# Packing the count stage's places two words to a stride, and dividing them apart on the engine

## The chip, the core and the metric

The kernel runs on one core of one Trainium2 chip. Its time is device microseconds from launch to the end of the program; a profiled execution gives beside it a span, from the first to the last recorded instruction. The engines are PE (TensorE, matrix multiplication; its weight loads are listed apart, as PEld), DVE (VectorE), ACT (ScalarE), POOL (GpSimd) and SP (SyncE, which issues DMAs). Each engine has a sequencer that reads its instructions in order. Register arithmetic and loads of registers run on that sequencer; the profile lists them under the engine's name with a q (PEldq, ACTq) and doesn't count them as busy time.

## The reference

Four graph layers run over one graph of 3125 nodes and 103,125 edges, sorted by destination. Each layer normalizes the node rows, applies a ReLU and adds its result to `x`:

```python
edge_index = jnp.stack([src, dst])
h = jnp.maximum(_layernorm(x, axis=-1), 0.0)
x = x + _L0_gnn_ref(h, edge_index, ...)        # gated messages summed over the edges, then a GRU
h = jnp.maximum(_layernorm(x, axis=-1), 0.0)
x = x + _L1_gnn_ref(h, edge_index)             # three hops of scatter-mean
h = jnp.maximum(_layernorm(x, axis=-1), 0.0)
x = x + _L2_gnn_ref(h, src, dst, ...)          # mean over the neighbours, then an MLP
h = jnp.maximum(_layernorm(x, axis=-1), 0.0)
x = x + _L3_gnn_ref(h, edge_index, ...)        # attention over the edges, feed-forward
return x
```

Layers 0 to 2 sum over the edges, as in

```python
msg_sum = jax.ops.segment_sum(feat[src], dst, num_segments=n)
```

and such a sum is a product with the matrix of counts, whose element for two nodes is the number of edges from one to the other. The kernel builds that matrix once, from `src` and `dst`.

## The kernel before

The program runs in blocks, one after the other, and an engine enters a block when all have left the one before. `tables` (L423) computes index tables on the chip. `count_matrix` (L679) builds the matrix of counts: this is the count stage. Then come the layers.

**The count stage.** The edges lie in 806 tiles of 128. The destinations are cut into windows of 5 nodes. A step is one tile against one window that it touches, and there are 1431 steps. For one step, PE multiplies a 128x128 matrix that is 1 where an edge's source has a given low part by a 128x125 matrix that is 1 where its destination in the window and the high part of its source match (L762). The product is added into a slot of PSUM of 128 f32 words that stands for the window. PSUM holds 32 slots (8 banks of 4), in 4 pairs of banks with 8 slots each. Eight steps are a stride (`STRIDE`), and there are 179 strides.

Three engines work on it side by side. DVE compares the tables for 16 steps at a time (L725, two instructions for two strides) and writes into a ring of three. PE takes, for each stride, first two one-column products that clear the flags of the pair of banks that comes next (`clear`, L740), and then the stride's eight products. ACT copies one finished pair of banks, 8 slots, from PSUM to `counts` for each stride (L769). PE waits at the head of stride j until ACT has made its first j - 1 copies. ACT waits until PE has counted stride j and until its own copy before is done.

**Which slot a step goes to depends on the data.** So the addresses stand in a table in SBUF, and the engine loads them into registers: `values` (L116 to L121) becomes one register load that fetches a run of words. The table is made in `CountTables.places` (L364 to L392) by DVE, inside `tables`, on one partition. `AHEAD` strides share a fetch. Before, `AHEAD` is 3: 27 words, filled up to 28, are fetched for three strides, in 60 fetches. 24 of them are ready addresses (slot number times 128), 3 are the pair to clear, times 1024. In front of each product, the sequencer turns a word into an address (a FUSED_REGOPS instruction, several register operations in one). ACT has a table of its own (`c_out`), with the pair in the high half of a word and the column in the low half, loaded 8 words at a time by `Registers.take`.

PE's loop: the fetch and the products stand in one queue, in the order of the code, with no fetch ahead of its first use.

Of the kernel before, what the change touches and what calls it, by code (L numbers as in the profile page):

```python
# [30 lines left out]
AHEAD = 3  # L31
# [186 lines left out]
class CountTables:  # L218
# [7 lines left out]
    def __init__(self, k, scope):  # L226
        s = k.s
        n, cols = s.csteps, s.nb * s.w
        self.k = k

        def sb(name, shape, dt=F32):
            return k.sb(scope, name, shape, dt, "right")
        self.key, self.low = sb("c_key", [P, n + 1], F16), sb("c_low", [P, n + 1], F16)


        self.fetches = -(-s.strides // AHEAD)
        self.words = -(-AHEAD * (STRIDE + 1) // 4) * 4
        self.place = sb("c_place", [1, self.fetches, self.words], I32)
        self.out = sb("c_out", [1, self.fetches * AHEAD], I32)
        self.lows, self.keys = sb("low_table", [P, P, 2], F16), sb("key_table", [P, cols, 2], F16)  # L240

    def stage(self, scope):
# [6 lines left out]
        def sb(name, shape, dt=F32):  # L249
            return k.sb(scope, name, shape, dt)  # L250
# [13 lines left out]
        self.window = sb("c_window", [1, whole], I32)  # L264
# [98 lines left out]
    def places(self, e):  # L363
# [3 lines left out]
        assert STRIDE * PAIRS == 32 and SLOT == 128  # L367
        wide = STRIDE * s.w
        every = AHEAD * STRIDE
        e.memset(self.place[:, :, every + AHEAD:], 0).then_inc(*v.up())  # L370
        e.tensor_scalar(self.place[:, :, 0:every], self.window[:, :].rearrange("p (a b) -> p a b", b=every),
                             STRIDE * PAIRS - 1, 7, ALU.bitwise_and, ALU.logical_shift_left).then_inc(*v.up())
# [3 lines left out]
        for to, more in ((self.clear, 1), (self.pair, PAIRS - 1)):  # L376
# [5 lines left out]
        e.tensor_scalar(self.place[:, :, every:every + AHEAD], self.clear[:, :].rearrange(  # L382
            "p (a b) -> p a b", b=AHEAD), PAIRS - 1, 10, ALU.bitwise_and, ALU.logical_shift_left).then_inc(*v.up())
# [8 lines left out]
        e.tensor_tensor(self.out[:, :], self.column[:, :], self.pair[:, :], ALU.bitwise_or).then_inc(*v.up())  # L392

# [285 lines left out]
def count_matrix(k, c, counts, room, nodes, w_nodes, factors):  # L679
# [10 lines left out]
    with ExitStack() as scope:  # L690
# [12 lines left out]
        flat = k.psum[:, :, :].rearrange("p b n -> p (b n)")  # L703

        with k.nc.Block() as block:
# [32 lines left out]
            def _(e):  # L738
                def clear(bank):
                    return e.matmul(bank, none[:, 0:P], none[:, 0:1], start=True, stop=True, skip_group_check=True)  # L740
                words = c.place[0:1, :, :].rearrange("p a b -> p (a b)")
                last_slot = (STRIDE * PAIRS - 1) * SLOT
# [5 lines left out]
                for j in range(s.strides):  # L748
                    if j % AHEAD == 0:
                        at = j // AHEAD * c.words  # L750
                        fetched = k.values(ENGINE.PE, words, at, at + c.words, last_slot)
                    place = fetched[j % AHEAD * STRIDE:(j % AHEAD + 1) * STRIDE]
                    ahead = fetched[AHEAD * STRIDE + j % AHEAD].with_bounds(min_val=0, max_val=(PAIRS - 1) * 1024)
                    if j >= 2:
                        e.wait_ge(copied.sem, copied.at(j - 1))
                    for i in range(2):
                        clear(flat[:, 512 * i + 511:][:, bass.ds(ahead, 1)])
                    if j % per == 0:
                        e.wait_ge(hots.sem, hots.at(2 * (j // per) + 2))
                    for i in range(j * STRIDE, min(s.csteps, (j + 1) * STRIDE)):  # L760
                        hot = (slice(None), i // keep % ring, i % keep // 2, slice(None), i % 2)
                        last = e.matmul(flat[:, bass.ds(place[i - j * STRIDE], cols)], lows[hot], keys[hot], start=False, stop=True,  # L762
                                        skip_group_check=True)
# [3 lines left out]
            def _(e):  # L767
# [6 lines left out]
                for j in range(s.strides):  # L774
                    if j % 8 == 0:
                        out = outs.take(j)
                    pair = (out[j % 8] >> 16).with_bounds(min_val=0, max_val=PAIRS - 1)
                    column = (out[j % 8] & 0xffff).with_bounds(min_val=0, max_val=wide * (s.fills - 2))
# [1989 lines left out]
```

## Time and profile before

| what | value |
|---|---|
| time, median of 3 runs | 2528.77 us (2525.51 to 2531.3) |
| span of the profiled execution | 2249.7 us |
| median less span: launch and what lies around the span | 279.1 us |
| mean granted clock of TensorE | 0.829 |
| the count stage, in the span | 75 to 417.6 us |

The profiled execution has no time of its own beside its span; the difference of 279.1 us to the median of the runs stands in for what lies around it. In the rows below, times are microseconds from the span's start. "Idle before, releaser" is what ended the time in which an engine did nothing. The granted clock is a share of 2.4 GHz: 0.50 is 1.2 GHz.

### The profile page before, as it was taken

To read this page: it belongs to the slowest core of one execution; us is meant where nothing else is said; L and a number is where in the kernel's file an instruction comes from. 1 tells how busy PE (TensorE), PEld (TensorE's weight loads), DVE (VectorE), ACT (ScalarE), POOL (GpSimd) and SP (SyncE) were. 2 spreads that over 40 slices of the span, in tenths; PEclk is the share of its full clock that TensorE was granted. 3 is DMA by queue.
4 is the path that set the end of the run, shared out by engine and by line. 5 is a ranking of instruction groups with operands and counts; after the bars stand their busy time and mean duration, and the time that the engine had idled before them with its cause. 6 is when DMAs were issued, how large, how long until landed. Compare 5 with 4: busy or idle time off the path is not lost. (4 is left out here: it accounts for less than half of the span.)

```text
span 2249.7 us, 34161 instructions
## 1 busy us (share of the span) xinstructions
PE 1665.0 (74%) x10041; PEld 1359.7 (60%) x10041; DVE 1504.7 (67%) x3141; ACT 969.8 (43%) x2263; POOL 916.3 (41%) x880
## 2 busy tenths in 40 slices
PE   5566666899799999865667677766777767776756
PEld 2455555655478887634566666666666656666744
DVE  4766666577744342477677777867777867787875
ACT  0355565677455234430234434434434335344535
POOL 1000000000100000037777777777777777777800
PEclk9555555799999999988788988888888898898877
DMA  2100000000034000034333333333343333333211
GB/s 70 60 1 1 1 1 1 8 0 0 29 87 130 27 1 6 14 100 96 92 90 91 97 93 91 92 96 92 87 100 94 86 95 97 91 93 93 60 39 29
DMA packets 134433, 136.86 MB, mean 61 GB/s; under 512 B 28689, under 2 KB 105074, under 8 KB 134258
## 3 DMA queue, kind: packets, MB, share of 16 engines
q0 software_dynamic: 27776, 60.71, 12.2%
q1 hardware_dynamic: 106482, 73.98, 11.5%
q8 instruction: 90, 1.47, 0.3%
q14 instruction: 85, 0.70, 0.1%
HBM read 129.67 MB, written 4.92 MB: 60 GB/s over the span
## 5 line engine op out<-in xcount | busy, mean ns | idle before, releaser
L2112 POOL DMA_INDIRECT rows<-x_l,src x856 | 896.9, 1048 | 292.5 <-issue 260.1
L2180 PE MATMUL psum<-both,node_hot 128*128 128x144 f32 x1712 | 304.1, 332 | 202.0 <-DVE both L2374 175.2
L2180 PEld LDWEIGHTS psum<-both,node_hot 128*128 128x128 f32 x1712 | 264.7, 222 | 229.4 <-issue 197.4
L2127 PE MATMUL psum<-w_e,edges 128*128 128x272 f32 x856 | 323.9, 466 | 56.7 <-DVE z L2287 46.9
L2129 PEld LDWEIGHTS psum<-x_r,hot 128*128 128x128 f32 x1712 | 313.8, 224 | 51.1
L2129 PE MATMUL psum<-x_r,hot 128*128 x1712 | 313.1, 312 | 0.0
L2287 DVE TENSOR_TENSOR z<-psum,rows 128x544 f32<-128x544 f32 x214 | 154.3, 721 | 235.4 <-issue 163.7
L2237 ACT ACTIVATE apart<-iota,minus_rel 128x128 f32<-128x128 f32 x828 | 261.9, 386 | 0.0
L769 ACT ACTIVATE counts<-psum (+1 forms) x181 | 181.5, 1003 | 175.8 <-PE psum L762 112.1
L1145 POOL TENSOR_TENSOR ht<-ht,mix_rows 128x512 f32<-128x512 f32 (+1 forms) x7 | 7.8, 1149 | 587.4 <-ACT mix_rows L1186 587.4
L1260 PE MATMUL psum<-halves,counts 128*128 128x257 f16 (+1 forms) x1725 | 198.1, 277 | 7.4 <-DVE halves L1465 3.9
L762 PE MATMUL psum<-keys,x 128*128 128x125 f16 x1431 | 201.3, 283 | 0.4
L2127 PEld LDWEIGHTS psum<-w_e,edges 128*128 128x128 f32 x856 | 160.7, 228 | 62.4 <-DVE hot L2280 31.2
L1260 PEld LDWEIGHTS psum<-halves,counts 128*128 128x128 f16 (+1 forms) x1725 | 171.2, 100 | 34.3 <-DVE halves L1465 4.5
L725 DVE TENSOR_TENSOR x<-low_table,c_low 128x2048 f16<-128x2048 f16 x90 | 109.6, 1218 | 116.0 <-PE psum L762 114.6
L762 PEld LDWEIGHTS psum<-keys,x 128*128 128x128 f16 x1431 | 148.3, 104 | 25.8 <-issue 1.6
L2392 DVE TENSOR_TENSOR acc<-acc,psum 128x144 f32 x428 | 128.6, 300 | 44.9 <-PE psum L2180 8.0
L2233 ACT ACTIVATE both<-weight 128x64 f32<-128x64 f32 x214 | 52.9, 247 | 235.7 <-PE psum L2180 232.8
L2300 DVE TENSOR_REDUCE alpha<-z 128x32 f32<-128x544 f32 x214 | 152.5, 713 | 1.5 <-issue 0.3
L2293 DVE SCALAR_TENSOR_TENSOR z<-z,att 128x512 f32<-128x512 f32 x214 | 146.5, 685 | 1.1
L2374 DVE TENSOR_TENSOR both<-rows,weight 128x512 f32<-128x512 f32 x214 | 143.9, 680 | 0.2 <-ACT weight L2224 0.2
L740 PE MATMUL psum<-none 128*128 128x1 f16 x366 | 57.1, 183 | 105.7 <-ACT counts L769 102.1
(335 smaller groups left out, 2187.3 us busy)
## 6 DMA issues: line engine op xcount, KB each, us to landing
rel_row<-e_rel_rows SPq DMA_DIRECT2D x107, 256.0 KB
edges<-edge_t SPq DMA_DIRECT2D x428, 32.0 KB
rows<-x_l,src POOLq DMA_INDIRECT x856
edge_part<-edge_t SPq DMA_DIRECT2D x40, 320.0 KB, 3.1
x_r<-x_l SPq DMA_DIRECT2D x1, 1632.0 KB
ht<-x SPq DMA_DIRECT2D x6, 256.0 KB, 2.8
new<-e_new_before SPq DMA_DIRECT2D x12, 128.0 KB
new<-e_new_behind SPq DMA_DIRECT2D x12, 128.0 KB
```

The lines of the kernel that those rows point to most:

```text
L762: last = e.matmul(flat[:, bass.ds(place[i - j * STRIDE], cols)], lows[hot], keys[hot], start=False, stop=True, skip_group_check=True)
L769: return e.activation(counts[:, :, column].rearrange("p h (a j) -> p h a j", j=w), pair.rearrange("p b (a n) -> p (b a) n", n=SLOT)[:, 0:f ...
L1260: last = e.matmul(ps, counts[:, i, b * P:b * P + rows], halves[:, i, :], start=i == 0, stop=i == s.nb - 1)
L2112: e.indirect_dma_start(rows[:, g % ring, j * ROW:(j + 1) * ROW], None, k.xl, bass.IndirectOffsetOnAxis(ap=src[:, at:at + 1], axis=0)).then ...
L2127: e.matmul(pair[:, j // 2, :], edges[:, r, :], w_e[:, j:j + 2, :].rearrange("p j f -> p (j f)"), start=True, stop=False)
L2129: final = e.matmul(pair[:, j // 2, j % 2 * ROW:(j % 2 + 1) * ROW], hot[:, two, j * P:(j + 1) * P], node_rows[j // 2], start=False, stop=j ...
L2180: final = e.matmul(to, near_hot[:, at, j, :], both[:, at, j, :], start=j % 2 == 0, stop=j % 2 == 1)
L2237: e.activation(apart[:, u % 2, j, :], iota[:, :], ACT.Abs, bias=minus_rel[:, 4 * u + j:4 * u + j + 1]).then_inc(*far.up())
L2287: e.tensor_tensor(z[:, g % 2, :].rearrange("p (b f) -> p b f", b=2), pair_of(g), rows_at(g).rearrange("p (b f) -> p b f", b=2), ALU.add).t ...
L2293: e.scalar_tensor_tensor(heads, heads, 0.0, att_of(k, 4), ALU.max, ALU.mult).then_inc(*leaky.up())
L2300: e.tensor_reduce(alpha[:, b.two, :, g - b.first, :], z[:, g % 2, :].rearrange("p (v h c) -> p v h c", v=4, h=HEADS), AX.X, ALU.add).then_ ...
L2374: e.tensor_tensor(both[:, at, :, 0:D].rearrange("p v (h c) -> p v h c", c=CH), rows_at(u).rearrange("p (v h c) -> p v h c", v=4, h=HEADS)[ ...
```

## The change

Two words per stride replace nine. Each holds four slot numbers in base 32 (`SLOTS` = 32, `HALF` = 4), and the first also the pair to clear, above them. The values stay under 2 to the 24th. DVE packs them by multiplying and adding (`scalar_tensor_tensor`). `AHEAD` becomes 8, so 16 words are fetched for eight strides, and 23 fetches serve 179 strides. In front of each product, the sequencer takes the slot out of the word by a division, a remainder or both (`slot_of`); the pair to clear is a division too. The PSUM views are taken in bytes. On ACT the shift and the mask become a division and a remainder. No product, copy or comparison changes.

```diff
--- before.py
+++ after.py
@@ -28,7 +28,9 @@
 SLOT = 128
 STRIDE = 2 * IN_BANK
 PAIRS = 4
-AHEAD = 3
+AHEAD = 8
+SLOTS = BANKS * IN_BANK
+HALF = STRIDE // 2
 F16_SCALE = 4096.0
 
 
@@ -234,8 +236,8 @@
 
 
         self.fetches = -(-s.strides // AHEAD)
-        self.words = -(-AHEAD * (STRIDE + 1) // 4) * 4
-        self.place = sb("c_place", [1, self.fetches, self.words], I32)
+        self.words = 2 * AHEAD
+        self.place = sb("c_place", [1, self.fetches * AHEAD, 2], I32)
         self.out = sb("c_out", [1, self.fetches * AHEAD], I32)
         self.lows, self.keys = sb("low_table", [P, P, 2], F16), sb("key_table", [P, cols, 2], F16)
 
@@ -261,7 +263,7 @@
         self.ones = sb("ones", [P, 1], F16)
         strides = self.fetches * AHEAD
         whole = strides * STRIDE
-        self.window = sb("c_window", [1, whole], I32)
+        self.window, self.slot = sb("c_window", [1, whole], I32), sb("c_slot", [1, strides, 2, HALF], I32)
         self.fill, self.early = sb("c_fill", [1, strides], I32), sb("c_early", [1, strides])
         self.clear, self.pair, self.column = (sb(x, [1, strides], I32) for x in ("c_clear", "c_pair", "c_column"))
         self.blank, self.dst_here, self.src_here, self.numbers_here, self.tables_here = (k.flag(x) for x in (
@@ -364,12 +366,11 @@
 
 
         s, v = self.k.s, self.v
-        assert STRIDE * PAIRS == 32 and SLOT == 128
+        assert STRIDE * PAIRS == SLOTS and SLOTS ** HALF * PAIRS < 1 << 24
         wide = STRIDE * s.w
-        every = AHEAD * STRIDE
-        e.memset(self.place[:, :, every + AHEAD:], 0).then_inc(*v.up())
-        e.tensor_scalar(self.place[:, :, 0:every], self.window[:, :].rearrange("p (a b) -> p a b", b=every),
-                             STRIDE * PAIRS - 1, 7, ALU.bitwise_and, ALU.logical_shift_left).then_inc(*v.up())
+        slot, place = self.slot, self.place
+        e.tensor_scalar(slot[:, :, :, :].rearrange("p a h b -> p (a h b)"), self.window[:, :], SLOTS - 1, None,
+                             ALU.bitwise_and).then_inc(*v.up())
         e.tensor_scalar(self.fill[:, :], self.window[:, ::STRIDE], 3, None, ALU.logical_shift_right).then_inc(*v.up())
         t = v.n
         e.wait_ge(v.sem, v.at(t))
@@ -379,8 +380,9 @@
                                  ALU.is_lt, ALU.mult).then_inc(*v.up())
         t = v.n
         e.wait_ge(v.sem, v.at(t))
-        e.tensor_scalar(self.place[:, :, every:every + AHEAD], self.clear[:, :].rearrange(
-            "p (a b) -> p a b", b=AHEAD), PAIRS - 1, 10, ALU.bitwise_and, ALU.logical_shift_left).then_inc(*v.up())
+        e.tensor_scalar(self.clear[:, :], self.clear[:, :], PAIRS - 1, None, ALU.bitwise_and).then_inc(*v.up())
+        e.scalar_tensor_tensor(place[:, :, :], slot[:, :, :, HALF - 1], float(SLOTS), slot[:, :, :, HALF - 2],
+                                        ALU.mult, ALU.add).then_inc(*v.up())
         e.tensor_scalar(self.pair[:, :], self.pair[:, :], PAIRS - 1, 16, ALU.bitwise_and, ALU.logical_shift_left).then_inc(*v.up())
         e.scalar_tensor_tensor(self.early[:, :], self.fill[:, :], float(wide), self.early[:, :],
                                         ALU.mult, ALU.add).then_inc(*v.up())
@@ -390,6 +392,13 @@
         t = v.n
         e.wait_ge(v.sem, v.at(t))
         e.tensor_tensor(self.out[:, :], self.column[:, :], self.pair[:, :], ALU.bitwise_or).then_inc(*v.up())
+        for b in range(HALF - 3, -1, -1):
+            e.scalar_tensor_tensor(place[:, :, :], place[:, :, :], float(SLOTS), slot[:, :, :, b],
+                                            ALU.mult, ALU.add).then_inc(*v.up())
+            t = v.n
+            e.wait_ge(v.sem, v.at(t))
+        e.scalar_tensor_tensor(place[:, :, 0], self.clear[:, :], float(SLOTS ** HALF), place[:, :, 0],
+                                        ALU.mult, ALU.add).then_inc(*v.up())
 
     def tensor(self, e):
         s, kb, bank = self.k.s, self.kb, self.k.bank
@@ -700,7 +709,6 @@
 
         stats_at, moments_at, root_at, factors_at, rows_at = 4, 29, 64, 38, 90
         assert moments_at == stats_at + s.nb and factors_at < chunks and rows_at + 2 * s.nb < s.strides
-        flat = k.psum[:, :, :].rearrange("p b n -> p (b n)")
 
         with k.nc.Block() as block:
             @block.sync
@@ -739,7 +747,20 @@
                 def clear(bank):
                     return e.matmul(bank, none[:, 0:P], none[:, 0:1], start=True, stop=True, skip_group_check=True)
                 words = c.place[0:1, :, :].rearrange("p a b -> p (a b)")
-                last_slot = (STRIDE * PAIRS - 1) * SLOT
+                in_bytes = k.psum[:, :, :].rearrange("p b n -> p (b n)").bitcast(mybir.dt.uint8)
+                by_slot, by_pair = (in_bytes.rearrange("p (a n) -> p a n", a=q) for q in (SLOTS, PAIRS))
+
+                def places_in(view, at, lo, n):
+                    return view[:, bass.ds(at, 1), 4 * lo:4 * (lo + n)].rearrange("p o n -> p (o n)").bitcast(F32)
+
+                def slot_of(pair_of_words, i):
+                    half, b = divmod(i, HALF)
+                    x = pair_of_words[half]
+                    if b:
+                        x = x // SLOTS ** b
+                    if half == 0 or b < HALF - 1:
+                        x = x % SLOTS
+                    return x.with_bounds(min_val=0, max_val=SLOTS - 1)
                 e.wait_ge(consts.sem, consts.at(1))
                 for i in range(BANKS):
                     e.matmul(k.bank[i], none[:, 0:P], none[:, :], start=True, stop=True, skip_group_check=True)
@@ -748,18 +769,18 @@
                 for j in range(s.strides):
                     if j % AHEAD == 0:
                         at = j // AHEAD * c.words
-                        fetched = k.values(ENGINE.PE, words, at, at + c.words, last_slot)
-                    place = fetched[j % AHEAD * STRIDE:(j % AHEAD + 1) * STRIDE]
-                    ahead = fetched[AHEAD * STRIDE + j % AHEAD].with_bounds(min_val=0, max_val=(PAIRS - 1) * 1024)
+                        fetched = k.values(ENGINE.PE, words, at, at + c.words, SLOTS ** HALF * PAIRS - 1)
+                    place = fetched[2 * (j % AHEAD):2 * (j % AHEAD) + 2]
+                    ahead = (place[0] // SLOTS ** HALF).with_bounds(min_val=0, max_val=PAIRS - 1)
                     if j >= 2:
                         e.wait_ge(copied.sem, copied.at(j - 1))
                     for i in range(2):
-                        clear(flat[:, 512 * i + 511:][:, bass.ds(ahead, 1)])
+                        clear(places_in(by_pair, ahead, 512 * i + 511, 1))
                     if j % per == 0:
                         e.wait_ge(hots.sem, hots.at(2 * (j // per) + 2))
                     for i in range(j * STRIDE, min(s.csteps, (j + 1) * STRIDE)):
                         hot = (slice(None), i // keep % ring, i % keep // 2, slice(None), i % 2)
-                        last = e.matmul(flat[:, bass.ds(place[i - j * STRIDE], cols)], lows[hot], keys[hot], start=False, stop=True,
+                        last = e.matmul(places_in(by_slot, slot_of(place, i - j * STRIDE), 0, cols), lows[hot], keys[hot], start=False, stop=True,
                                         skip_group_check=True)
                     last.then_inc(*counted.up())
 
@@ -774,8 +795,8 @@
                 for j in range(s.strides):
                     if j % 8 == 0:
                         out = outs.take(j)
-                    pair = (out[j % 8] >> 16).with_bounds(min_val=0, max_val=PAIRS - 1)
-                    column = (out[j % 8] & 0xffff).with_bounds(min_val=0, max_val=wide * (s.fills - 2))
+                    pair = (out[j % 8] // 65536).with_bounds(min_val=0, max_val=PAIRS - 1)
+                    column = (out[j % 8] % 65536).with_bounds(min_val=0, max_val=wide * (s.fills - 2))
                     if j:
                         e.wait_ge(counted.sem, counted.at(j))
                         e.wait_ge(copied.sem, copied.at(j))
```

## Rows read from the trace of the kernel before

**Rows 1.** Busy time by stretch: stretch, length, engines, granted clock, DMA share, GB/s.

```profile
75.00:417.60 342.60, 233.84 (x1805) 186.48 (x1805) 215.77 (x234) 192.07 (x208) 0.00 (x0) 0.51 0.02 6
79.00:85.00 6.00, 4.05 (x41) 3.14 (x39) 5.84 (x6) 4.02 (x4) 0.00 (x0) 1.00 0.72 250
96.00:416.00 320.00, 219.19 (x1696) 176.13 (x1694) 198.82 (x215) 180.55 (x196) 0.00 (x0) 0.50 0.00 1
416.00:434.00 18.00, 15.30 (x89) 13.08 (x90) 10.48 (x54) 12.16 (x34) 0.00 (x0) 0.79 0.09 23
```

**Rows 2.** Waits, 79 to 416 us: engine, line, released by; us, times, longest.

```profile
PEld psum L740 <- issue: 117.2, 64, 2.1
DVE x L725 <- PE psum L762: 114.6, 67, 2.3
ACT counts L769 <- PE psum L762: 112.1, 68, 2.2
PE psum L740 <- ACT counts L769: 102.1, 57, 1.9
ACT counts L769 <- ACT counts L769: 33.7, 93, 0.6
```

**Rows 3.** Line 119, register loads: count, ns min/median/max, first and last start.

```profile
L119 PEldq TENSOR_LOAD <-c_place x60: 1869/1873/2092, 75.9 to 411.4; - x60
L119 PEldq TENSOR_LOAD <-regs x54: 334/589/1008, 981.0 to 2099.2; - x54
L119 ACTq TENSOR_LOAD <-c_out x23: 538/547/752, 75.4 to 393.8; - x23
```

**Rows 4.** Line 119 from 2090 to 2110 us, the last load of that loop.

```profile
L119 PEldq TENSOR_LOAD <-regs x1: 334/334/334, 2099.2 to 2099.2; - x1
```

**Rows 5.** Timeline of weight loads, 86 to 99.5 us: start, us, line, count, idle before.

```profile
89.66 0.23 PEld L740 LDWEIGHTS psum<-none 128*128 128x128 f16 x2 [1.96 <-issue]
90.92 0.23 PEld L740 LDWEIGHTS psum<-none 128*128 128x128 f16 x2
91.22 0.92 PEld L762 LDWEIGHTS psum<-keys,x 128*128 128x128 f16 x8
92.19 0.23 PEld L740 LDWEIGHTS psum<-none 128*128 128x128 f16 x2
95.34 0.23 PEld L740 LDWEIGHTS psum<-none 128*128 128x128 f16 x2 [1.96 <-issue]
```

**Rows 6.** The same timeline, 79 to 85 us.

```profile
79.11 0.48 PEld L762 LDWEIGHTS psum<-keys,x 128*128 128x128 f16 x8
79.63 0.90 PEld L762 LDWEIGHTS psum<-keys,x 128*128 128x128 f16 x8
```

**Rows 7.** Register operations of the stage's lines, over the whole span.

```profile
L762 PEldq FUSED_REGOPS  x1431: 37/37/42, 78.3 to 415.5; - x179
L740 PEldq FUSED_REGOPS  x358: 46/51/51, 78.1 to 414.6; - x179
L769 ACTq ALU_OP  x179: 35/35/38, 79.4 to 414.9; - x179
L769 ACTq FUSED_REGOPS  x350: 42/65/88, 85.3 to 415.0; - x175
```

**Rows 8.** Line 2129 in the attention: products and the register operations before them.

```profile
L2129 PE MATMUL psum<-x_r,hot x1712: 279/279/434, 989.5 to 2137.1; 128*128 x191
L2129 PEldq FUSED_REGOPS  x428: 46/46/51, 988.4 to 2134.1; - x143
```

**Rows 9.** Timeline of ACT, 84 to 100 us.

```profile
92.75 1.01 ACT L769 ACTIVATE counts<-psum  x1 [0.35 <-ACT counts L769]
94.11 1.00 ACT L769 ACTIVATE counts<-psum  x1 [0.35 <-ACT counts L769]
```

**Rows 10.** Timeline of DVE, 54 to 62 us: `places` and what follows it.

```profile
54.47 0.86 DVE L371 TENSOR_SCALAR c_place<-c_window 1x1440 int32<-1x1440 int32 x1
56.19 0.24 DVE L382 TENSOR_SCALAR c_place<-c_clear 1x180 int32<-1x180 int32 x1
56.52 0.33 DVE L385 SCALAR_TENSOR_TENSOR c_early<-c_fill,c_early 1x180 f32<-1x180 int32 x1
56.88 0.24 DVE L389 TENSOR_SCALAR c_column<-c_early 1x180 int32<-1x180 f32 x1
57.43 0.15 DVE L494 TENSOR_SCALAR first<-e_window 128x4 f32<-128x4 f32 x1
```

**Rows 11.** Line 725, DVE's comparisons: count, ns min/median/max.

```profile
L725 DVE TENSOR_TENSOR x<-low_table,c_low x90: 693/1225/1227, 75.8 to 406.0; 128x2048 f16<-128x2048 f16 x89, 128x1024 f16<-128x1024 f16 x1
L725 DVE TENSOR_TENSOR keys<-key_table,c_key x90: 675/1193/1196, 76.9 to 406.6; 128x2000 f16<-128x2000 f16 x89, 128x1000 f16<-128x1000 f16 x1
```

## The prediction

> **What bounds the kernel now.** I forecast 2554 us, some 26 us slower. First the stretches. The count stage takes 342.6 of the span's 2249.7 us, and no engine is full in it: PE 233.8, DVE 215.8, ACT 192.1 us [rows 1]. So the next view is of waits. DVE and ACT wait 115 and 112 us for PE's products, which means that both are ahead of PE. PE's weight loads wait 117 us in 64 pieces, "issue" being the cause: no semaphore held them [rows 2]. The row that lays PE's next wait on ACT (102 us, 57 times) has the same pieces: they are of 1.96 us, and at each the engine had long been free to go on. What fills them is in the list of register loads: 60 loads of the place table, 1.873 us each, 28 words [rows 3]. The timeline shows the period: clears at 89.66 and again at 95.34 us, so 5.68 us for three strides, one gap of 1.96 us in each [rows 5]. A load adds 1.935 us: 1.96 less the 0.025 or so that lie before a weight load anyway (two clears' loads, at 0.10 each, take 0.23). So three strides take 3.745 us and one takes 1.248.
>
> And what sets those 1.248 us? A stride's eight weight loads take 0.90 us at the full granted clock and 0.92 at half of it [rows 1, 5, 6]. Less the last load's own 0.1 us, over seven steps, that is a pitch of 115 ns at both clocks. The eight just before, which had queued up behind the initial clears, went through in 0.48 us, or 54 ns a piece [rows 6]. So the array could go on faster; what comes to it every 115 ns is the sequencer's output, and 37 ns of the 115 are the FUSED_REGOPS in front of each product [rows 7]. PE's sequencer bounds the stage, in its loads and in its register operations alike. The check: 179 x 1.248 = 223.4 us and 59 loads x 1.935 = 114.2 us (the first load ran beside the initial clears), together 337.6; the rows run from 78.1 to 415.6, so 337.5 [rows 7].
>
> By the Trainium skill ("Advanced Engine Details and Errata", Clock Domains), PE's sequencer is not behind the array's clock gate. The trace agrees: 115 ns at granted clocks of 1.00 and of 0.50.
>
> **The loads removed.** A load of 8 words on PE took 0.589 us, the last one of that loop 0.334 (it has 4 words, 428 being 53 x 8 + 4), one of 28 words 1.873 [rows 3, 4]. From 4 to 8 words it is 64 ns a word, from 8 to 28 also 64. So 16 words take 0.589 + 8 x 0.064 = 1.10 us, and a load adds 1.16. The first is hidden again; 22 x 1.16 = 25.5 us. Removed: 114.2 - 25.5 = **88.7 us**. ACT's 8 words took 0.547 us [rows 3], so the price is not PE's alone. Bounds: 0.589 and 1.873 us for 16 words give savings of 100 and 71.6 us, but the straight line through three sizes leaves a few us at most.
>
> The Trainium skill speaks otherwise ("Runtime: NRT & Kernel Launch", The ~15µs preamble/postamble breakdown): there a register load is one round trip to memory for a few words. If the words cost nothing, each new load would take 1.873 us as well, the saving would be 71.6 us and the whole 17 us slower still. The rows of 4, 8 and 28 words speak against it.
>
> **The register operations added.** Before, the sequencer multiplies a ready word by a constant and adds a base. After, of the eight slots of a stride, six need a division (those at places 1, 2, 3 of either word) and seven a remainder (all but the last of the second word, which has nothing above it). That is 13 more operations in the fused instructions of a stride. The clears need the pair: one division, used by both. That an expression is worked out once and kept shows in the attention, where 1712 products at two addresses for every four have only 428 FUSED_REGOPS [rows 8]. So 14; 15 if it is done twice.
>
> The price: PE's trace shows neither division nor remainder. The nearest rows are ACT's, in front of its copies. There two FUSED_REGOPS go with each copy, a short one of 42 ns and a long one of 88, the long with the mask on the column, the short without [rows 7]; the even mix has its median halfway, at 65. So one such operation costs 88 - 42 = 46 ns on ACT. PE's own rows bound it from below: 51 ns at L740 against 37 at L762 is 14 ns for whatever more the clear's address holds [rows 7]. From above: an operation by itself took 35 ns on ACT [rows 7] and some 27 more until the next, 62. I take 45 ns, by the row of the same kind of work. 14 x 45 = 0.63 us a stride, x 179 = **112.8 us added**. All of it lies on the path: the sequencer is in order, the array and the other engines are ahead of it. The pitch of a product goes from 115 to about 190 ns, and a stride from 1.248 to 1.88.
>
> No other engine comes near. ACT's copies can follow each other at 1.36 us (92.75 to 94.11) [rows 9], DVE needs 1.225 + 1.193 for two strides [rows 11]. Both are below the new 1.88. ACT's division and remainder in place of shift and mask: perhaps one instruction fewer, perhaps 20 ns more; hidden under PE's stride either way, down to a stride of 1.36 us.
>
> **Packing on DVE.** The copy with shift and mask (0.86 us, 1440 elements) stays in kind; L382 stays. Added are four `scalar_tensor_tensor`, three over 368 elements and one over 184, each waiting for the one before. Such a one over 180 took 0.33 us, its follower starting 0.36 later [rows 10]; with 368 I take 0.43. One runs among others, and a memset goes. So +1.6 us, before DVE goes on at L494 with the tables that end the block. On the path; bounds 0 and 2.5.
>
> **The clock.** The stage runs at a granted 0.50 [rows 1]. PE's sequencer doesn't mind, so within the stage neither a rise nor a fall changes the time. Behind it, the 18 us from 416 are at 0.79 on the mean. I take them as they are; were the clock full from the start, 18 x 0.21 = 3.8 us would be the most to win, and as much is there to lose.
>
> **The sum.** 112.8 - 88.7 + 1.6 = +25.7 us. The span goes from 2249.7 to 2275.4; with the 279.1 us around it, which I keep, that is 2554.5 us against a median of 2528.8.
>
> **The rivals.**
> *Cheap operations, faster.* If a division costs in a fused instruction what the more in L740 costs, 14 ns, a stride is 1.44 us: 14 x 14 x 179 = 35.1 us added, and the sum is -52, or 2477 us. It turns at (88.7 - 1.6) / (14 x 179) = 35 ns per operation; below that, the kernel is faster. For it: 14 ns is PE's own row. Against: ACT's 46 is of the same kind of work, and dividing is not adding.
> *The operations don't fuse.* Each is an instruction with its own gap: 62 ns by ACT; on PE, where 78 of the 115 ns are the other two instructions of a product and the gaps, I estimate 37 + 78 / 2 = 76 ns. 14 x 62 x 179 = 155, so +68, 2597 us; at 76, +103, 2632 us. For it: ACT's shift is such a lone ALU_OP [rows 7]. Against: its mask is not.
> *The load's price is per load.* Were each new load as long as an old one, the saving would be 71.6 us and the time 2571.6 us; for it speaks nothing but the many words of the one long row, against it the row of 4 words.
> *The release of the clock.* By the Trainium skill ("TensorE: Matmul & The Clock Gate", What's actually happening) the array's clock follows recent activity; the long gaps go, so it could be released. In this kernel that would be worth at most the 3.8 us behind the stage, by the pitch that was the same at both clocks.
>
> **How the numbers follow.** The forecast's case has 0.77: its own range is 38 to 52 ns an operation and 14 or 15 of them, +8 to +53, so 2537 to 2582. Cheap or nearly so (under 33 ns, 2477 to 2524) 0.12; not fused 0.07; per-load price 0.04. Here 0.2%, or 5 us, is what can be told from no change. Faster 0.13, the same 0.06, slower 0.81. The range of 8 in 10 takes in the clock, the per-load price and a slightly cheaper operation: 2528 to 2590.
>
> **What would show it.** 23 register loads of the table, near 1.10 us each. FUSED_REGOPS at L762 with three or four lengths instead of one: 37 or so, about 82 (one more operation) and about 127 (two more), the most of 127. Clears 1.88 us apart within a fetch. ACT's and DVE's waits for PE grow, ACT by 0.5 us a stride less its former share. The stage ends near 443 us instead of 417.6. I am wrong if the fused instructions stay under 70 ns, if lone ALU_OPs stand before the products, or if the stage runs at ACT's pitch of 1.36 us.

## The result: 0.7% slower, and the profile after

The changed kernel took 2547.12 us (median of 4 runs, 2541.56 to 2553.45) against 2528.13 of the kernel before beside it (4 runs): a ratio of 1.0073, 95% interval 1.005 to 1.0097, or +19.0 us (12.6 to 24.5). Forecast were 2554, or +25.7. Later the two were timed again on a chip on which both are quicker (two kinds of chip are told apart below): 2261.74 (6 runs) against 2245.69 (17), ratio 1.0070 (1.0050 to 1.0089), +16.0 us. The sign and the mechanism held; one term of the sum, the register operations, was some 9 us too large.

First the stage by stretches; the columns are those of [rows 1]. Below it, the table's loads and the register operations of its lines, which answer to [rows 3, 7]; the first of these rows is of 93 to 434 us, the others of the whole span.

```profile
77.70:433.60 355.90, 328.62 (x1805) 184.36 (x1805) 216.24 (x234) 192.44 (x208) 0.00 (x0) 0.51 0.02 6
...
L121 PEldq TENSOR_LOAD <-c_place x22: 1101/1104/1122, 94.8 to 425.5; - x22
...
L783 PEldq FUSED_REGOPS  x1431: 73/115/136, 80.4 to 431.8; - x179
L748 PEldq FUSED_REGOPS  x179: 77/82/86, 79.5 to 430.3; - x179
L748 PEldq ALU_OP  x179: 32/32/42, 79.7 to 430.5; - x179
L790 ACTq FUSED_REGOPS  x358: 42/90/153, 81.6 to 430.8; - x179
```

Lines L783, L748 and L790 are L762, L740 and L769 of before. There are 23 loads of 1.10 us where there were 60 of 1.87, and the median register operation of a product went from 37 to 115 ns. The granted clock is 0.51 as it was. PE's busy time rose from 234 to 329 us with the same 1805 instructions: the work is the same, and the weight loads' sum is unchanged (186 and 184 us), so I read it as records that last longer, not as a fuller array.

The timeline of PE's weight loads shows the new period (columns of [rows 5]):

```profile
96.14 0.20 PEld L748 LDWEIGHTS psum<-none 128*128 128x128 f16 x2 [1.24 <-issue]
96.40 1.44 PEld L783 LDWEIGHTS psum<-keys,x 128*128 128x128 f16 x8
97.90 0.19 PEld L748 LDWEIGHTS psum<-none 128*128 128x128 f16 x2
98.17 1.46 PEld L783 LDWEIGHTS psum<-keys,x 128*128 128x128 f16 x8
99.68 0.19 PEld L748 LDWEIGHTS psum<-none 128*128 128x128 f16 x2
```

Eight products go out in 1.44 us instead of 0.92. The gap for a load is 1.24 us, and it comes once in eight strides. From the rows of L748: the clears run from 79.5 to 430.3 us, that is 178 strides with 22 loads in them. A load adds 1.157 us by the gaps between the clears' register operations, so a stride takes (350.8 - 25.5) / 178 = 1.828 us. Before it took 1.248. The waits, 79 to 433 us, against [rows 2]:

```profile
ACT counts L790 <- PE psum L783: 158.6, 177, 2.2
DVE x L733 <- PE psum L783: 129.4, 85, 2.6
...
PEld psum L748 <- issue: 27.1, 23, 1.3
```

The "issue" row shrank from 117 to 27 us, with 23 pieces instead of 64. This row alone would suggest 90 us won. What was added is in no row of waits: it lies between one weight load and the next, too short for the view to list, and shows only in the longer waits of ACT (112 to 159 us) and DVE (115 to 129) for PE and in the table of register operations.

The balance of the two traces, worked out from the load count of the stage and the strides' lengths (no view prints it):

```
                          before            after            difference
179 strides               179 x 1.248       179 x 1.828      +103.8 us
loads on the path          59 x 1.936        22 x 1.157       -88.8 us
start of the stage         75.51             77.76              +2.3 us
end of the stage          417.85            433.94             +16.1 us
```

The three terms make +17.3; the 1.2 us to +16.1 lie in the first and last strides.

**The chips.** The span is 2540.0 us in an execution that took 2541.7. So only 1.7 us lie around a span, and the 279 us that the prediction put around that of before were not that. The attention (a later stage of the program) accounts for them. Its stretch, first from the changed kernel's first profile and then from its second, on the quicker chip:

```profile
1000.00:2450.00 1450.00, 869.08 (x4488) 760.62 (x4489) 885.71 (x1769) 445.73 (x1346) 884.32 (x856) 0.77 0.30 75
```

```profile
1002.00:2166.00 1164.00, 823.31 (x4475) 727.99 (x4476) 885.97 (x1762) 444.91 (x1338) 890.61 (x856) 0.85 0.38 93
```

The same program takes some 280 us more here in the one than in the other, with DVE and POOL equally busy. Two chips ran the kernel before in 2245.7 and 2246.8 us (here called the quick kind) and one in 2525.3 (the slow kind). By its span of 2249.7 us the profile of before was of the quick kind; by their 2528 us its timed runs were of the slow kind. The count stage is alike on both (356.2 and 356.6 us after, 342.3 and 342.8 before), so the balance above stands.

### The profile page after: what moved, and what is told of

The parts are those of the page before. It is cut to its first block and busy times, and to the rows that moved or that the text cites. A ratio compares the mean times of both kernels' runs of the same rounds, so it can differ in the third digit from the quotient of the medians.

```text
span 2540.0 us, 33948 instructions
## 1 busy us (share of the span) xinstructions
PE 1806.1 (71%) x10041; PEld 1391.9 (55%) x10041; DVE 1503.3 (59%) x3144; ACT 969.2 (38%) x2263; POOL 904.2 (36%) x880
## 3 DMA queue, kind: packets, MB, share of 16 engines
q0 software_dynamic: 27776, 60.71, 10.4%
## 5 line engine op out<-in xcount | busy, mean ns | idle before, releaser
L2133 POOL DMA_INDIRECT rows<-x_l,src x856 | 884.7, 1034 | 556.8 <-issue 267.6
L2201 PE MATMUL psum<-both,node_hot 128*128 128x144 f32 x1712 | 329.2, 351 | 342.6 <-DVE both L2395 224.1
L2201 PEld LDWEIGHTS psum<-both,node_hot 128*128 128x128 f32 x1712 | 288.2, 239 | 374.5 <-issue 322.1
L2148 PE MATMUL psum<-w_e,edges 128*128 128x272 f32 x856 | 333.8, 476 | 114.4 <-issue 66.8
L2150 PEld LDWEIGHTS psum<-x_r,hot 128*128 128x128 f32 x1712 | 320.1, 228 | 95.1 <-issue 44.5
L2150 PE MATMUL psum<-x_r,hot 128*128 x1712 | 326.6, 317 | 36.0 <-issue 35.5
L783 PE MATMUL psum<-keys,x 128*128 128x125 f16 x1431 | 294.3, 283 | 2.1
L2301 DVE TENSOR_SCALAR hot<-rel_row,place 128x512 f32<-128x512 int16 x214 | 103.5, 484 | 322.5 <-remote 256.8
L790 ACT ACTIVATE counts<-psum (+1 forms) x181 | 181.5, 1003 | 191.8 <-PE psum L783 158.6
L2148 PEld LDWEIGHTS psum<-w_e,edges 128*128 128x128 f32 x856 | 168.7, 237 | 119.6 <-issue 74.7
L783 PEld LDWEIGHTS psum<-keys,x 128*128 128x128 f16 x1431 | 148.4, 104 | 129.7 <-issue 7.7
L2230 ACT ACTIVATE line<-psum 1x128 f32<-1x128 f32 (+2 forms) x30 | 7.5, 249 | 363.5 <-DMA cols<-L_gnn_ln_b 167.2
```

The costliest lines, as they stand in the source:

```text
L783: last = e.matmul(places_in(by_slot, slot_of(place, i - j * STRIDE), 0, cols), lows[hot], keys[hot], start=False, stop=True, skip_group_ch ...
L790: return e.activation(counts[:, :, column].rearrange("p h (a j) -> p h a j", j=w), pair.rearrange("p b (a n) -> p (b a) n", n=SLOT)[:, 0:f ...
L2133: e.indirect_dma_start(rows[:, g % ring, j * ROW:(j + 1) * ROW], None, k.xl, bass.IndirectOffsetOnAxis(ap=src[:, at:at + 1], axis=0)).then ...
L2148: e.matmul(pair[:, j // 2, :], edges[:, r, :], w_e[:, j:j + 2, :].rearrange("p j f -> p (j f)"), start=True, stop=False)
L2150: final = e.matmul(pair[:, j // 2, j % 2 * ROW:(j % 2 + 1) * ROW], hot[:, two, j * P:(j + 1) * P], node_rows[j // 2], start=False, stop=j ...
L2201: final = e.matmul(to, near_hot[:, at, j, :], both[:, at, j, :], start=j % 2 == 0, stop=j % 2 == 1)
```

## The experiments

Each kernel is told by its edit (the code is abridged), against the kernel before where nothing else is said. All but the two marked ones ran on chips of the quick kind, beside runs of the kernel before at 2246.83 or 2245.69 us. "Stage" is from DVE's first instruction of it to the next block's first DMA: 342.8 us for the kernel before.

**The kernel before, looked at again**, for the 279 us.

> The kernel before, unchanged, profiled once more. The profile shown of it has a span of 2249.7 us, its timed runs took 2528 us, and the changed kernel's profile has 2540.0 us with 2541.7 us measured. The count stage should repeat to within 1 us (342.6 us from barrier to barrier). For the rest of the span, either 2250 again (then the profile and the timed runs differ by some 276 us by the profiling itself) or about 2526 (then the first profile was an odd execution, and its attention stage, 1195 us long, will be some 275 us longer here).

It took 2247.73 us, with a span of 2244.9 and a stage of 342.8: the short attention is repeated in a timed run. So the profile of before was not odd; the runs of the first comparison were the slower ones. That the chip makes the difference is read from the times of three chips; no kernel was timed on one chip in both ways.

**The loads alone.** The after kernel's table and fetches, but the two words of a stride hold ready addresses, used by four products each, so nothing is divided. What it leaves out: the true places.

```
+AHEAD = 8
+self.words = 2 * AHEAD
-flat[:, bass.ds(place[i - j * STRIDE], cols)]
+flat[:, bass.ds(place[(i - j * STRIDE) // HALF], cols)]
+k.nc.disable_value_cache = True   # so that each product keeps its own register ops
```

> The fetches alone: two words per stride, 16 words for eight strides, but each word is a ready address, so the register operations in front of each product and each clear are those of the kernel before (2 and 3 in a fused instruction). It leaves the slot numbers of single steps out: the four products of half a stride go to one slot, so its sums are not the reference's. Theory, a register load costs by the word and PE's sequencer bounds the stage: 23 loads of 1.10 us each, stage shorter by 88.7 us (342.6 to 254), time 2528 to about 2440. Rival, a price per load: 1.87 us each, shorter by 71.6 us, 2456. Rival, other engines bound before that is reached: ACT can copy every 1.36 us, 179 x 1.36 = 243, so ACT should not bind yet, but if it does the gain stops near -80 us.

2158.82 us, ratio 0.9611 (0.9585 to 0.9638): -88.0 us, stage -86.5. Its loads and its products' operations:

```profile
L121 PEldq TENSOR_LOAD <-c_place x23: 1101/1105/1293, 75.5 to 324.3; - x23
...
L764 PEldq FUSED_REGOPS  x1431: 37/37/42, 77.8 to 329.0; - x179
```

With the operations at their old 37 ns, a stride without a load took 1.261 us, and a load added 1.21. The term of the loads, 88.7 us, is right.

**The operations alone.** 28 words for three strides as before, but each word is stored shifted by five bits more where the after kernel divides, and PE takes it apart: six divisions and seven remainders a stride, the clears' code untouched. What it leaves out: the fewer words.

```
+if i % 4: x = x // 32
+if i < 7: x = x % 4096
```

> The register operations alone: 28 words for three strides, as before, but six of a stride's eight words are stored times 32 and divided by 32, and seven get a remainder by 4096 that changes nothing: 13 operations more per stride, all in the fused instructions. Theory, 41 ns for a remainder and 48 for a division, as the changed kernel's fused instructions suggest, all on the path: 7 x 41 + 6 x 48 = 575 ns a stride, 179 strides, +103 us less a few that the gaps of instruction fetch gave back, so +95 to +103, about 2626. Rival, cheap operations (14 ns): +33 us, 2561. Rival, the sequencer is not the bound when the array is busy: below +50.

2347.43 us, ratio 1.0448 (1.0417 to 1.0479): +100.6 us, stage +99.5.

```profile
L119 PEldq TENSOR_LOAD <-c_place x60: 1870/1873/2088, 76.0 to 510.6; - x60
...
L771 PEldq FUSED_REGOPS  x1431: 75/116/133, 78.4 to 515.8; - x179
```

A stride took 1.806 us, 0.558 more than before, or 43 ns for each of 13 operations (11 of the 558 ns stand at the first clear, whose instruction took 62 ns instead of 51; nothing here tells why). Loads and operations add up: -88.0 + 100.6 = +12.6, the clears (0.022 x 179 = 3.9) and the later start (2.3) make it +18.8, and measured were +16.0 (11.2 to 20.0) on the same kind of chip.

**The load's price.** Two strides to a fetch, so 20 words, 90 times.

```
-AHEAD = 3
+AHEAD = 2
```

> The kernel before with two strides to a fetch in place of three: 90 loads of 20 words (18 and two of padding) in place of 60 loads of 28. Theory, by the word: 20 words take 0.589 + 12 x 0.064 = 1.36 us and add 1.42; 89 x 1.42 = 126.3 against 114.2 us, +12 us, 2540. Rival, by the load: 89 x 1.935 = 172 us, +58, 2586.

```profile
L119 PEldq TENSOR_LOAD <-c_place x90: 1356/1359/1576, 76.2 to 424.5; - x90
```

1.359 us against 1.36 expected; 2254.95 us, ratio 1.0042 (1.0028 to 1.0056), +8.1, where 12 were expected; the stage, 353.2 us, is 10.4 longer. A price per load would have cost 58. With 4, 8, 16 and 28 words at 0.334, 0.589, 1.104 and 1.873 us there are now five sizes on one line, 64 ns a word; all five are multiples of four words.

**The changed kernel again.**

> The changed kernel, once more, beside the kernel before on one chip on which the latter took 2246.8 us. In the first comparison both were some 280 us longer, all of it in the attention. Theory: the change adds to the count stage and to the tables before it alone, so the difference in microseconds stays and its share grows a little: the parts measured by themselves are -88.0 us for the fetches and +100.6 for 13 of the 14 operations; with +2.25 for the packing and about +1 for the clears that is +16, 2263 us, ratio 1.007. Rival: part of the +19 us of the first comparison came from the attention, then less than +12 here or clearly another number.

+16.0 us, as told above. In the trace the stage is 356.6 us.

**Shifts and masks in place of division and remainder**, against the after kernel, on PE and ACT.

```
-x = x // SLOTS ** b
+x = x >> (5 * b)
-x = x % SLOTS
+x = x & (SLOTS - 1)
```

> The changed kernel with shifts and masks in place of divisions and remainders, the same values. The fused instruction takes neither, so most become instructions of their own in front of the product's. Theory: a lone operation takes 32 ns and a step of 60 to the next; 13 of them in a stride are 780 ns in place of some 555, so +40 us against the changed kernel, about 2303. Rival: a shift is so much simpler than a division that it is cheaper even alone: no change or faster than the changed kernel.

2382.24 us, ratio 1.0611 (1.0587 to 1.0635) against the kernel before, +136.5; +120 over the after kernel, three times what I expected.

```profile
L783 PEldq ALU_OP  x2148: 32/36/41, 79.6 to 553.2; - x196
L783 PEldq FUSED_REGOPS  x1431: 37/37/78, 79.7 to 553.3; - x179
```

Of the 13 operations of a stride's products 12 are instructions of their own (2148 = 12 x 179): the masks, and the shifts that stand with one. Only the shift that has no mask behind it, at the last place of the second word, is in the fused instruction, and there the compiled program has a division after all; the shift for the clears is one too. Of the others each takes 32 or 36 ns, and some 96 ns pass from its start to the next register operation. I had put 60 ns, which in the changed kernel is the time from the clears' lone addition to the weight load behind it, not to the next register operation.

**Packed words with three strides a fetch**, against the after kernel.

```
-AHEAD = 8
+AHEAD = 3
```

> The changed kernel with three strides to a fetch in place of eight: 60 loads of 6 words in place of 23 of 16. Theory: 6 words take 0.334 + 2 x 0.064 = 0.46 us and add 0.52; 59 x 0.52 = 30.7 us against 22 x 1.16 = 25.5, so +5 us against the changed kernel, about 2268. Rival: what counts is the number of loads: 37 more of over 1 us each, +40 or more.

2304.94 us, ratio 1.0270 (1.0246 to 1.0294) against the kernel before: +59, and +43 over the after kernel instead of +5. The loads of six words, all of them and then two neighbours alone:

```profile
L121 PEldq TENSOR_LOAD <-c_place x60: 813/1248/1493, 78.5 to 472.6; - x60
...
L121 PEldq TENSOR_LOAD <-c_place x1: 1475/1475/1475, 99.3 to 99.3; - x1
...
L121 PEldq TENSOR_LOAD <-c_place x1: 814/814/814, 106.2 to 106.2; - x1
```

Six words at 64 ns were to take 0.46 us. They take 0.82 and 1.48 in turns. The fetches begin at word 0, 6, 12, and so on, so every second one begins in the middle of four aligned words. With about 0.078 us for the load, 0.255 for four words together and 0.24 for a word by itself: 0.078 + 0.255 + 2 x 0.24 = 0.81, and six single words are 1.52. So a load that began between fours went word by word, though words 8 to 11 of the second fetch are an aligned four: where it begins decides, which the expectation of the next kernel doesn't say. That kernel was made to try the whole fours.

**The same with aligned fetches.** As the last, but each fetch of three strides fills a row of eight words (two of them zeros). It ran on a chip of the slow kind, beside the kernel before at 2525.28 us.

```
-self.words = 2 * AHEAD
+self.words = -(-2 * AHEAD // 4) * 4
```

> Packed words with three strides to a fetch, as in the run before (6 words, 2305 us, loads of 0.82 and 1.48 us in turns), but each fetch's words filled up to 8, so that every load starts at a multiple of four words and takes whole fours. New theory: a load costs by accesses, some 0.255 us for four words that start at a multiple of four and some 0.24 us for each word that doesn't lie in such a four, on top of 0.08. Then each load takes 0.59 us and adds 0.65, 59 x 0.65 = 38 us against 22 x 1.16 = 25.5 in the changed kernel: +13, and up to +2 for more packing instructions, 2275 us. Rival: what made those loads slow is their number or what surrounds them, 60 between heavier fused instructions: about 2305 again.

```profile
L121 PEldq TENSOR_LOAD <-c_place x60: 587/590/782, 80.2 to 441.8; - x60
```

Eight words are 0.590 us: more words, in less time than either kind of the six-word loads. 2554.92 us, ratio 1.0131 (1.0093 to 1.0169) or +29.6; expected were +29. The stage is 368.1 us, 12 more than with 16 words. So a load that begins at a multiple of four costs by fours, and a word that is left over costs about as much as four. This run changed the start and the length at once; the part of the start alone is shown by the two kinds of six-word loads.

**One product for both clears.** The kernel before, with its clears addressed through a view by pairs of banks in bytes, as the after kernel does: the pair's number times 4096 serves both, and only the second's base is added anew.

```
-... PAIRS - 1, 10, ALU.bitwise_and, ALU.logical_shift_left)
+... PAIRS - 1, None, ALU.bitwise_and)
-clear(flat[:, 512 * i + 511:][:, bass.ds(ahead, 1)])
+clear(by_pair[:, bass.ds(ahead, 1), 4 * (512 * i + 511):...].bitcast(F32))
```

> A version meant to beat both: the kernel before with its 28 ready words for three strides, but the pair to clear is kept as a number and the two clears are taken from one view by pairs, so that the second reuses the product of the first: a fused instruction with a multiplication and an addition, and then a lone addition, in place of two fused instructions of three operations. Theory: the changed kernel's trace has 32 ns for that lone addition and a step of 60 to what follows, where a fused one of 51 takes a step of 129. So the clears take 115 + 89 = 204 ns in place of 258, 54 ns less a stride, 179 strides: -9.7 us, ratio 0.9957. Rival: the clears wait for ACT's copy anyway, no change.

```profile
L740 PEldq FUSED_REGOPS  x179: 37/37/42, 77.5 to 407.2; - x179
L740 PEldq ALU_OP  x179: 32/32/42, 77.6 to 407.3; - x179
```

2239.9 us (12 runs) against 2245.69, ratio 0.9973 (0.9962 to 0.9985): -5.8 us, where 9.7 were expected; the stage, 335.6 us, is 7.2 shorter. It beats both kernels, by 0.3% the one before. The two operations shrank from 2 x 51 to 37 + 32 ns, 33 in all, and the clears' pitches from 2 x 129 to 115 + 112, which is 31 ns instead of the 54 expected: after the lone addition the next register operation started 52 ns after the weight load's start, not 29. A whole stride gained 40 ns by the medians (1.228 to 1.188 us), the rest of it because the instructions of the first two products took 37 ns instead of 42; no run tells why. 40 ns x 179 = 7.2 us.

**The stage without its register bound.** As the loads alone, but the four products at one address share its register operations. It ran on a chip of the slow kind beside 2525.28 us, twice; it leaves out the true places as well.

> The fetches alone once more (two ready words per stride; it leaves the slot numbers of single steps out, so four products go to one slot), but now the four products of half a stride also share one register address, so six of a stride's eight fused instructions are gone. PE's sequencer would need some 0.84 us a stride. Theory: then PE's sequencer isn't the bound any more; ACT's copies are, at 1.36 us each, 179 x 1.36 = 243 us for the stage, against some 254 with all fused instructions: 2150 us. Rival: the bound is PE all along, in the array at half its clock: 8 x 0.105 + 2 x 0.105 = 1.05 us a stride, 188 + 25 us, 2110.

2440.84 us, ratio 0.9671 (0.9633 to 0.971): -84.4 us (-93 to -73), where 97 were expected. The whole time doesn't tell it from the -88.0 of the loads alone; the stage does, with 248.8 us against 256.3. ACT's timeline:

```profile
89.14 1.01 ACT L770 ACTIVATE counts<-psum  x1 [0.34 <-PE psum L763]
90.48 1.01 ACT L770 ACTIVATE counts<-psum  x1 [0.34 <-ACT counts L770]
91.83 1.01 ACT L770 ACTIVATE counts<-psum  x1 [0.34 <-PE psum L763]
93.18 1.01 ACT L770 ACTIVATE counts<-psum  x1 [0.34 <-PE psum L763]
```

A copy every 1.345 us and 0.34 between two: ACT is the next bound. Its pitch x 179 = 240.8 us. The gap is named as a wait for PE in most rows, but its length is the same where it is named ACT, and also where a load of 1.10 us lies in PE's stride. Work on the sequencer thus pays until a stride with its share of loads is down to 1.35 us; the loads alone left it at 1.261 + 1.21 / 8 = 1.41.

PE's weight loads in the same kernel, at a granted clock of 0.50:

```profile
100.44 0.76 PEld L763 LDWEIGHTS psum<-keys,x 128*128 128x128 f16 x8
```

Eight went in 0.76 us where the kernel before takes 0.92, and from the third on they started 102 to 106 ns apart.

## Why the prediction was right, and by which steps

**What bounds the stage.** Right. Operations added to PE's sequencer and words taken from it moved the time one for one (+100.6 and -88.0 us) at an unchanged granted clock (0.50 from 96 us to the stage's end), while the array did the same work. How far the array was ahead was read too generously: the 54 ns a product were of a stretch at a granted clock of 1.00. At 0.50 the kernel with the shared address has some 105 ns, only 10 less than the sequencer's 115. The forecast added operations, so this did it no harm; one that took operations from the products would have met the array after 10 ns a product.

**The loads.** Right: 1.10 us predicted and 1.104 measured, 88.7 us against 88.8 in the trace and 88.0 alone. But "64 ns a word" was drawn through 4, 8 and 28 words, all of them multiples of four. The six-word loads showed that it is some 256 ns for four words together, and about as much for one by itself.

**The operations.** 112.8 us predicted, 103.8 found: this is the term that was off. Of its two factors the price was near, 45 ns against 43. The count was not. Thirteen of the fourteen cost 0.558 us a stride; the fourteenth, the division for the clears, cost 0.580 - 0.558 = 0.022. The two kernels' own traces split it alike: between 96 and 400 us the mean pitches of a stride's products grew by 0.555 us and those of its clears by 0.022. The view by pairs took an addition from the first clear, and the second reuses the product. That needs 82 + 32 ns [the rows of L748 above], where the old clears needed 2 x 51 [rows 7]. I counted what the new expression has more and did not set the whole new address beside the old one. The experiment with the shared product shows such a saving in the kernel before, 31 ns at the clears of a stride.

**How the price was found.** By luck in part. The compiled program has the constants of each instruction (of the two clears of before the first is shown; the second adds 1023):

```
PE before   product       load * 4, + 33554432
            clear         load + 511, * 4, + 33554432
PE after    product       load / 32^b, % 32 (one or both), * 512, + 33554432
            first clear   load / 1048576, * 4096, + 33556476
            second clear  product of the first + 33558524
ACT before  fused, long   load / 65536, * 2, * 512, * 4, + 33554432
            alone         load & 65535
            fused, short  * 2, + 31008
```

On ACT the lone operation was the mask and the long fused one held the shift, as a division, with two more multiplications. The prediction had mask and shift the other way round, and 88 - 42 = 46 ns was the price of three operations, not one. On PE, by the lengths of [rows 7] and of this kernel: one addition more is 51 - 37 = 14 ns; an instruction with a remainder (the product at the lowest place of a word) took 78 to 84, so 41 to 47 more, one with a division 85 to 87, 48 to 50 more, and one with both 112 to 136. The predicted lengths were 37, 82 and 127; the first never occurs, since each product has at least one of the two.

**The rivals.** Cheap operations fell: 43 ns, where the turning point was 35. Operations that don't fuse fell for this kernel, since division and remainder fuse. The shifts and masks showed the case itself: 96 ns a piece where the prediction had 76. The price per load fell with the 20 words. The clock had no part: 0.50 within the stage, and from the stage's end to the attention's first product of this kind (L2129 of before) 571.6 us before and 571.0 after. The Trainium skill ("Runtime: NRT & Kernel Launch", The ~15µs preamble/postamble breakdown) tells of one round trip for a few words where registers are loaded from HBM, around a kernel. The place table lies in SBUF, so the prediction applied the sentence to a case that it isn't about, and no run here tests it. The loads of this table took 1.873, 1.359, 1.104 and 0.59 us for 28, 20, 16 and 8 words.

**The packing.** DVE's timeline, against [rows 10]:

```profile
55.98 0.78 DVE L384 SCALAR_TENSOR_TENSOR c_place<-c_slot 1x368 int32<-1x368 int32 x1
...
57.77 1.62 DVE L396 SCALAR_TENSOR_TENSOR c_place<-c_place,c_slot 1x368 int32<-1x368 int32 x2
59.42 0.34 DVE L400 SCALAR_TENSOR_TENSOR c_place<-c_clear,c_place 1x184 int32<-1x184 int32 x1
59.70 0.15 DVE L503 TENSOR_SCALAR first<-e_window 128x4 f32<-128x4 f32 x1
```

Three operations over 368 elements took 0.8 us each where I had put 0.43: the time more than doubled with twice the elements (0.34 for 184). They read `c_slot` at every fourth word, where the row of 0.33 us read words side by side. In the kernel with aligned fetches, where they read every eighth, both kinds stand at 180 elements:

```profile
58.72 0.33 DVE L391 SCALAR_TENSOR_TENSOR c_early<-c_fill,c_early 1x180 f32<-1x180 int32 x1
...
59.62 1.78 DVE L401 SCALAR_TENSOR_TENSOR c_place<-c_place,c_slot 1x180 int32<-1x180 int32 x4
```

There one with the step took 0.47 us against 0.33 without. That speaks for the step as a part of the cause, but no run changed it alone. DVE goes on at 59.70 instead of 57.43, 2.27 us later, and the stage starts 2.25 later; 1.6 was predicted, with 2.5 as the bound.

**The stage's end.** At 433.9 us, where the text had "near 443". The terms of the prediction give 417.6 + 25.7 = 443.3; of the 9.4 us between, 9.0 are the term of the operations, the packing is 0.7 the other way, and 1.1 are the ends of the stage.

**The time around the span.** 279.1 us were a wrong reading that did no harm, since the sum was a difference and the added and removed work is of the same length on both kinds of chip. Left open is why the attention differs by 280 us between chips: the rows of the longer one name "remote" (a cause that the quick one's don't have; 257 us at one line of DVE) and more "issue", and no experiment here went after it.

## What to carry to other kernels

Where an in-order sequencer feeds an array that waits for it, words and operations are one budget. Here a word that came in an aligned four cost 64 ns, a division or remainder within a fused instruction 43, and a shift or mask that did not fuse 96. Packing saved 28 / 3 - 2 = 7.3 words a stride, 0.50 us with the load's own gap, and paid 14 operations, 0.58 us. Better than packing is an address that two instructions share, and a fetch that begins and ends at a multiple of four words. Count the operations of the whole address before and after, not those of the new expression, and take the constants of the compiled instructions before pricing them by a neighbour.

## What was unexpected of the hardware

- A register load of six words took 0.82 or 1.48 us, by where it began, and one of eight words that began at a multiple of four 0.59.
- After a register operation of 32 to 36 ns that stood alone, PE's next one started 96 ns after its start; a division or remainder in a fused one cost 41 to 50.
- At a granted clock of 0.50, products with register operations of 37 ns came every 115 ns and those whose address stood ready every 105.
- From the attention's start (1002 and 1000 us) to its end the same program took 1259 us in one profile and 1540 in another, on chips of the two kinds, its count stage the same to 0.5 us.
